# The sum of x and the bias in a two-layer kernel is made by VectorE instead of GpSimd

## The reference, cut to what matters

```python
# layer 0
att = softmax(gelu(gelu(cond @ W0 + b0) @ W1 + b1) @ W2 + b2)          # 32 x 8
y   = einsum('boi,bih->boh', einsum('bk,koi->boi', att, weight), x) + (att @ bias_k)[:, :, None]
x1  = x + (y @ kernel + bias + lora(y) + lora_shared(y))
# layer 1
c   = grouped_conv1d(x1, 9 taps, 4 groups) + (cond @ c_weight.T + fside)[:, :, None]
g   = c @ w12.T + b12
out = x1 + (silu(g1) * g2) @ w3.T + b3
```

## Time and profile before

| | us |
|---|---|
| median of 3 runs | 786.55 |
| lowest and highest | 785.95 and 787.77 |
| the profiled execution | 787.26 |
| its span | 785.4 |
| PE busy | 775.7 |
| DVE busy | 520.3 |
| ACT busy | 216.0 |
| POOL busy | 81.4 |

### The profile page before, as it was taken

How to read it: one execution, slowest core, us unless ns; L and a number is a source line. 1 busy time by engine, 2 the same in 40 slices (tenths; PEclk the granted TensorE clock), 3 DMA queues, 4 the chain that set the end, 5 groups by cost and what they waited for, 6 DMA issues and landing times.

```text
span 785.4 us, 10561 instructions
## 1 busy us (share of the span) xinstructions
PE 775.7 (99%) x3981; PEld 658.1 (84%) x3981; DVE 520.3 (66%) x624; ACT 216.0 (28%) x254; POOL 81.4 (10%) x54
## 2 busy tenths in 40 slices
PE   7999999999999999999999999999999999999998
PEld 6898888888888999978888888888888888888886
DVE  4966853543545679977777769777755896555552
ACT  4741110010010114143333336333333831111110
POOL 3250623223223000000000000000000000000000
PEclk9999999999999999999999999999999999999999
DMA  8969654563585795535553042488852854444441
GB/s 233 301 211 272 183 124 113 124 151 102 126 196 166 189 301 162 151 102 142 140 141 94 27 188 80 136 239 234 235 201 80 310 198 161 161 160 163 170 170 59
DMA packets 90515, 131.46 MB, mean 167 GB/s; under 512 B 10696, under 2 KB 69944, under 8 KB 87792
## 3 DMA queue, kind: packets, MB, share of 16 engines
q1 hardware_dynamic: 87552, 129.67, 54.9%
q10 hardware_dynamic: 2752, 1.12, 0.6%
q0 software_dynamic: 176, 0.21, 0.1%
HBM read 79.24 MB, written 51.72 MB: 167 GB/s over the span
## 4 chain that ended last, share of the span: by engine, by line
PE 93%; DMA 3%; DVE 1%; SPq 1%; ACT 1%; issue 1%; DVEq 0%
PE ps L1879 38%; PE ps L1620 37%; PE ps L1939 18%; DMA raw<-in_L_ffn_kernel 2%; DMA h_f<-h_scratch 1%; DVE wk_lo L1079 1%; SPq L398 0%; ACT wk_hi L815 0%; DVE res L1549 0%; ACT w_s_hi L898 0%; DVE w_a_lo L1282 0%; SPq L393 0%; DVE w_s_lo L1272 0%; DVE y_f L1130 0%; DVE hs_f L1518 0%
## 5 line engine op out<-in xcount | busy, mean ns | idle before, releaser
L1879 PE MATMUL ps<-cr,w_s_hi 128*128 128x512 f32 x512 | 157.7, 389 | 0.0
L1879 PE MATMUL ps<-cr,w_a_hi 128*128 128x512 f32 x384 | 118.5, 390 | 1.1 <-DVE s L1401 1.1
L1879 PEld LDWEIGHTS ps<-cr,w_s_hi 128*128 128x128 f32 x512 | 96.1, 188 | 20.0
L1879 PE MATMUL ps<-cr,w_s_lo 128*128 128x512 f32 x256 | 99.6, 389 | 0.0
L1879 PEld LDWEIGHTS ps<-cr,w_a_hi 128*128 128x128 f32 x384 | 71.9, 188 | 16.4 <-issue 1.5
L1620 PE MATMUL ps<-wk_hi,y_hi 128*128 128x512 f32 x256 | 80.4, 395 | 0.6 <-DVE wk_lo L1079 0.4
L1620 PE MATMUL ps<-wk_lo,y_hi 128*128 128x512 f32 x256 | 79.0, 390 | 0.0
L1620 PE MATMUL ps<-wk_hi,y_lo 128*128 128x512 f32 x256 | 78.8, 389 | 0.0
L1162 DVE TENSOR_TENSOR x_t<-ps,x_t 128x1024 f32<-128x1024 f32 x16 | 19.5, 1223 | 88.1 <-PE ps L1620 88.1
L749 POOL TENSOR_TENSOR x_t<-x_in,f_bias 128x1024 f32<-128x1024 f32 x16 | 61.6, 3847 | 143.4 <-DMA x_scratch<-x_t 97.0
L1879 PE MATMUL ps<-cr,w_a_lo 128*128 128x512 f32 x192 | 74.7, 389 | 0.0
(11 more groups left out here) (185 smaller groups left out, 1247.7 us busy)
## 6 DMA issues: line engine op xcount, KB each, us to landing
x_scratch<-x_t SPq DMA_DIRECT2D x128, 64.5 KB, 2.6
x<-x_scratch SPq DMA_DIRECT2D x16, 516.0 KB, 4.9
x_in<-in_x SPq DMA_DIRECT2D x16, 512.0 KB, 6.0
r_scratch<-r_t SPq DMA_DIRECT2D x16, 512.0 KB, 3.4
h_scratch<-s SPq DMA_DIRECT2D x32, 256.0 KB, 2.4
h_f<-h_scratch SPq DMA_DIRECT2D x8, 1024.0 KB, 6.0
res<-r_scratch SPq DMA_DIRECT2D x16, 512.0 KB, 5.0
raw<-in_L_ffn_w SPq DMA_DIRECT2D x56, 128.0 KB, 4.4
```

The lines of the kernel that those rows point to most:

```text
L1879: last = pe.matmul(o, l, r, start=first and q == 0 and n == 0, stop=q == 3 and n == 2, skip_group_check=True)
```

## The change: what it does

The function `x_plus_bias` moves from POOL's program to DVE's. POOL keeps the gathers of LoRA A's columns, which now wait only for `z_mm`. In DVE's program the 16 calls stand at these places: tiles 0 and 1 behind the last part of wk_lo and ahead of tile 2's y; tile 2 behind the residuals of tiles 0 and 1; in the loop, each behind the `take_y` of a later tile and ahead of the next `take_x1`; tile 15 between the two halves of the first turn of w12. Each waits for its x, and from tile 2 on for the stores of the x1 that was in the buffer and for its residual. The wait for `y_lo_made` goes.

```diff
@@ POOL
-            def x_plus_bias(slot, s):
-                pool.tensor_tensor(blocks(x1_t[s]), x_in[slot][:, :].rearrange("p (b h q) -> p h q b", h=2, q=4), fb_v,
-                                   ALU.add).then_inc(xb_made, 1)
...
-            pool.wait_ge(fbias_in, 16)
-            for t in range(2):
-                pool.wait_ge(wk_lo_made, KT - 1 + t)
-                pool.wait_ge(x_loaded[t], 16)
-                x_plus_bias(t, t)
             with pool.Fori(0, 3) as i:
-                for k in range(4):
-                    if k in (0, 3):
-                        g = i * 2 + (2 if k == 0 else 3)
-                        pool.wait_ge(z_mm, i * 2 + (1 if k == 0 else 2))
-                        gather_la(g, 0 if k == 0 else 1)
-                    pool.wait_ge(x1_stored[k % 2], i * 256 + 128 * (k // 2 + 1))
-                    pool.wait_ge(r_made, i * 4 + k + 1)
-                    pool.wait_ge(x_loaded[(k + 2) % 4], i * 16 + (16 if k < 2 else 32))
-                    pool.wait_ge(y_lo_made, i * 8 + 2 * k + 8)
-                    x_plus_bias((k + 2) % 4, k % 2)
...
+                for k in range(2):
+                    pool.wait_ge(z_mm, i * 2 + k + 1)
+                    gather_la(i * 2 + k + 2, k)
@@ DVE
             wk_lo_part(7)
+            def x_plus_bias(slot, s, loaded, stored=None, residuals=None):
+                dve.wait_ge(x_loaded[slot], loaded)
+                if stored is not None:
+                    dve.wait_ge(x1_stored[s], stored)
+                    dve.wait_ge(r_made, residuals)
+                dve.tensor_tensor(blocks(x1_t[s]), x_in[slot][:, :].rearrange("p (b h q) -> p h q b", h=2, q=4), fb_v,
+                                  ALU.add).then_inc(xb_made, 1)
+
+            dve.wait_ge(fbias_in, 16)
+            for t in range(2):
+                x_plus_bias(t, t, 16)
             dve.wait_ge(bias_rest_loaded, 16)
             take_y(2, 1, 0)
...
             residual(0, 0, None)
             residual(1, 1, None)
+            x_plus_bias(2, 0, 16, 128, 1)
...
                 take_y(t + 2, 1 - k, 0)
+                x_plus_bias(2 * k + 1, 1, i * 16 + 16, i * 256 + 128 * k, i * 4 + 2 * k)
                 take_x1(t, 0)
                 residual(t, 0, i * 32 + 16 * k)
                 take_y(t + 3, 1 - k, 1)
+                x_plus_bias(2 - 2 * k, 0, i * 16 + 16 * (k + 1), i * 256 + 128 * (k + 1), i * 4 + 2 * k + 1)
                 take_x1(t + 1, 1)
...
             turn_w12(0, 0)
+            x_plus_bias(3, 1, 64, 128 * 7, 14)
             turn_w12(0, 1)
```

More of the change, by code:

```diff
@@ L743, in gather_shared @@
                     pool.tensor_copy(la_g[s][:, :, c0:c0 + RANK], src[:, :, NG * RANK:].bitcast(F32))
-            fb_v = f_bias[:, :].rearrange("p (b h q) -> p h q b", h=2, q=4)
-            def x_plus_bias(slot, s):
-                pool.tensor_tensor(blocks(x1_t[s]), x_in[slot][:, :].rearrange("p (b h q) -> p h q b", h=2, q=4), fb_v,
-                                   ALU.add).then_inc(xb_made, 1)
             pool.wait_ge(las_hi_made, 1)
@@ L759, in _ @@
             gather_la(1, 1)
-            pool.wait_ge(fbias_in, 16)
-            for t in range(2):
-                pool.wait_ge(wk_lo_made, KT - 1 + t)
-                pool.wait_ge(x_loaded[t], 16)
-                x_plus_bias(t, t)
-            with pool.Fori(0, 3) as i:
-                for k in range(4):
-                    if k in (0, 3):
-                        g = i * 2 + (2 if k == 0 else 3)
-                        pool.wait_ge(z_mm, i * 2 + (1 if k == 0 else 2))
-                        gather_la(g, 0 if k == 0 else 1)
-                    pool.wait_ge(x1_stored[k % 2], i * 256 + 128 * (k // 2 + 1))
-                    pool.wait_ge(r_made, i * 4 + k + 1)
-                    pool.wait_ge(x_loaded[(k + 2) % 4], i * 16 + (16 if k < 2 else 32))
-                    pool.wait_ge(y_lo_made, i * 8 + 2 * k + 8)
-                    x_plus_bias((k + 2) % 4, k % 2)
[L776 to L781, removed]
+            with pool.Fori(0, 3) as i:
+                for k in range(2):
+                    pool.wait_ge(z_mm, i * 2 + k + 1)
+                    gather_la(i * 2 + k + 2, k)
         @block.scalar
@@ L1196, in _ @@
             wk_lo_part(7)
+            fb_v = f_bias[:, :].rearrange("p (b h q) -> p h q b", h=2, q=4)
+            def x_plus_bias(slot, s, loaded, stored=None, residuals=None):
[8 more added lines that the diff above has]
+                x_plus_bias(t, t, 16)
             dve.wait_ge(bias_rest_loaded, 16)
@@ L1229, in _ @@
             take_y(14, 1, 0)
+            x_plus_bias(1, 1, 64, 128 * 6, 12)
             take_x1(12, 0)
@@ L1232, in _ @@
             take_y(15, 1, 1)
+            x_plus_bias(2, 0, 64, 128 * 7, 13)
             take_x1(13, 1)
```

## The result

| | before | after |
|---|---|---|
| median, us (22 executions each, lowest to highest) | 786.88 (785.95 to 788.39) | 788.62 (787.24 to 791.75) |
| the profiled execution, its span | 787.26, 785.4 | 788.15, 786.3 |
| PE, DVE, POOL busy, us | 775.7, 520.3, 81.4 | 775.7, 549.1, 22.9 |

The ratio is 1.0021, with a 95% interval of 1.0015 to 1.0028: the changed kernel is 1.2 to 2.2 us slower, 1.74 us by the medians. The prediction gave 787.5 against 786.55 of before, +0.95 us. 788.62 lies inside its range for 8 in 10 and 0.2 us above the narrower band of 786.6 to 788.4.

What follows compares the result with a forecast made beforehand. PE was taken as the bound, busy 775.7 of 785.4 us. Only tile 2's add cost anything, 0.95 us, taking the median from 786.55 to 787.5 us (786.6 to 788.4; 8 in 10: 786.0 to 789.8).

Steps and rivals of the forecast that it cites:

- The price of an add: Each add on DVE: 2.15 us, taken from the residual, with a range of 1.2 to 4.1 us.
- The upper bound of 4.1: Add on DVE with stepped inputs fetched in turn; the dear-add rival gave 788.4 to 789.8 us, chance 0.12.
- Part 1: Adds of tiles 0 and 1 ahead of tile 2's y: 4.3 us hidden in 5.04 us of DVE idling, cost 0.
- 2d - 5.04: Price to PE at tile 3's y, for adds of d us, if DVE's idling ahead of tile 2's y is too short.
- Part 2: Tile 2's add waits for tile 0's stores, delaying tile 4's y bias and so PE's tile 5 y by 0.95 us.
- median of 3.3 us: Median landing time of a store in that stretch; it put tile 0's last store at 77.3 us at the earliest.
- the rival of the late store: At tile 2's add: one us lost per us that tile 0's stores land after 77.6; slower after 79.1; chance 0.1.
- parts 1 and 2 don't add up: A PE late from the start finds tile 0's stores landing at the same time; only the dearer of both delays counts.
- Part 3: Tile 3's add waits for tile 1's stores, making x1 of tile 2 2.3 us later; PE asks later, no cost.
- Part 4: POOL's adds no longer stretch DVE's operations: 2.7 and 1.9 us of DVE time given back, worth nothing on PE's path.
- The rival that they matter: All 4.6 us of DVE time given back by the vanished POOL-DVE locks reach PE: 782.0 us, chance 0.05.
- Parts 5 and 6: Steady loop's adds end 2.8 us before x1 is due at the tightest; the last add fits between w12's turns; cost 0.

Runs made afterwards that it cites:

- e8: The changed kernel run again without any edit, on the same chip as three other runs; ratio 1.0022 against the kernel before.
- e1: The changed kernel with tile 2's add moved behind tile 4's y on DVE instead of ahead of it; ratio 0.9997 against the kernel before.
- e5: The changed kernel with the adds of tiles 0 and 1 each made twice; ratio 1.0069 against the kernel before.
- e4: The changed kernel with tile 2's add made twice in a row at its place; ratio 1.0064 against the kernel before.
- e6: The changed kernel with the loop's eight adds each made twice; ratio 1.0025 against the kernel before.
- e9: The changed kernel with tile 2's add made three times in a row at its place; ratio 1.0090 against the kernel before.
- e2: The changed kernel with only tile 2's add given back to POOL, the other 15 on DVE; ratio 1.0006 against the kernel before.
- e3: The kernel before with only the adds of tiles 0 and 1 moved to DVE; ratio 1.0001 against the kernel before.
- e7: The changed kernel with SP's load of tile 5's x moved behind the stores of tile 0's x1; ratio 1.0010 against the kernel before.
- e10: The kernel of e1 with tile 2's add made twice, behind tile 4's y; ratio 1.0007 against the kernel before.

## Why the prediction was right in kind and short in size

**The price of an add.** Taken at 2.15 us by the residual; measured 2.15. The upper bound of 4.1, two stepped inputs in turn, is out for this form.

**Part 1, the start: right.** 0.7 us to spare was computed, and 0.70 us of idling is left. That the two agree so well is partly luck, since 0.21 us was left in the profiles of e8 and e1: here too the cover is the difference of two times that move from execution to execution. With four adds (e5) the price formula 2d - 5.04 gave the gap, and missed what the gap does to the clock.

**Part 2, tile 2's add: right place and mechanism, mis-sized by half.** I had the add at 78.50, PE starting at 81.4 where it wanted 80.46, 0.95 us. It measured 1.87 in the profile. The difference of 0.92 has three pieces: the stores landed 0.48 us later (78.98); PE was 0.38 us earlier at that place than in the profile of before, and the landing did not follow it; and the steps from add to PE took 2.97 us where I had 2.9. The step that was mis-sized is this one: I took one execution's landing as the landing, and one execution's arrival of PE as its arrival, though the price is the difference of two things that are set by different engines. In the five profiles in which DVE waited for the stores with the add ahead of tile 4's y (after, e4, e6, e8, e9) it began between 77.96 and 78.98. The median of 3.3 us that I set against it fits no last store: in these five profiles those took 4.36 to 5.48 us from the end of the issue to the landing. So the loss has a spread of a microsecond by itself. Tile 5's y was late by 0.85 to 1.87 us in the three profiles with one add there (e6, e8, after), and the medians of the two sets of runs give 1.26 and 1.74. In the profile of after, the rival of the late store, to which I gave 0.1, was the largest of the three pieces; at 78.98 it stayed below the 79.1 that the rival named. How much of the medians it explains is not shown, since the landings of the timed executions are not known.

**That parts 1 and 2 don't add up: right** (e5 closes the second gap).

**Part 3, tile 3's add: right.** Begun at 83.78 where 83.4 was said, and x1 of tile 2 at 85.94.

**Part 4, the locks: right.** The stretched operations are gone after the change and there in e2 and e3, without a trace in the time. The rival that they matter (782.0) is out.

**Parts 5 and 6: right.** No gap of PE from 110 to 268 us, even with twice the adds (e6). The last add ran from 249.49 to 251.66, the second turn ended at 253.69 and x1 of tile 14 began at 255.16, on time.

**The chances.** +0.21% lies on my border of 0.2% between within and slower. I gave "within" 0.74 with the forecast only 0.6 us below that border, while the landing alone moves the result by that much; the chance of slower should have been near a half.

## What to carry to other kernels
Moving an operation from an idle engine to another moves its waits too: ask of each wait not how long the engine can spare but what stands behind it in the new queue, and place it behind the step that the bounding engine asks for next, as e1 does. An operation of 2.15 us cost nothing that could be measured at 15 places, and 1 to 2 us at the one where it stood between a DMA's landing and PE's next bank; once the cover there was used up, each further one cost its full length. Where a price is a difference between a DMA's landing and another engine's arrival, read both from several profiles, or give the range that their spread makes.

## What the runs showed of the hardware
- PE's clock: idling of 3.31 us (e5) and 4.67 us (e9) was followed by a granted clock of 0.50 of full speed in a 2 us slice and a y product that took 3.48 and 3.65 us instead of 1.95; behind idling of 0.70 to 2.68 us (e6, e8, after, e4) the windows around the gap show 1.00. The two longer waits thus cost 1.53 and 1.70 us over their own length. I had not counted that in the upper cases.
- In the timed executions of the changed kernel the three longest (790.29, 791.25 and 791.75 us) have mean granted clocks of 0.998, 0.998 and 0.997, the others 0.999 or 1.0. The same holds for the two longest of e8 and the four longest of e6: of 46 executions with one add ahead of tile 4's y bias, nine have 0.998 or less, and they are the nine longest (790.1 to 791.93). In e4, e5 and e9, where the wait is longer, 14 of 15 have 0.998 or less; in the 44 of e1, e3, e7 and e10, and in the 73 of the kernel before that ran beside the experiments, none has. A late landing that lets PE idle for long would do that; none of those nine was profiled, and e2, which has no gap in its profile, has one such execution of 12 (790.37, 0.998), so the cause stays open.
- An fp32 add with two SBUF inputs read at a step of eight floats takes the same on DVE (2.15 us) as the residual with one stepped input and a stepped output (2.17), and 1.75 times the `take_x1` of the same size (1.22), whose SBUF operands are not stepped (its other input comes from the banks).
